# Layer 0 attention: copies between maxima and exponents, routing roots for two batches at once, and every variance root as exp(-0.5 ln v) with a Newton step

## The chip, the cores and the metric

One core of one Trainium2 chip runs the whole program. The metric is the device time of one execution in microseconds (us); lower is better. The unchanged kernel takes 1991.19 us, the median of three runs (1990.56 to 1992.09).

## The reference, cut to what matters

Four layers, each a gated cross attention and then a gated mixture of experts, over 8 batches of 256 tokens with 256 features:

```python
x = x + tanh(g_xattn[n]) * attention_n(layernorm(x), ctx)
x = x + tanh(g_ffn[n])   * experts_n(layernorm(x))
def _layernorm(x, axis=-1, eps=1e-05):
    return (x - m) / jnp.sqrt(v + eps)       # m, v: mean and variance over the features
# layer 0 attention: 16 heads of 16 features, a mask of its own for each batch
scores = jnp.einsum('bhqd,bhkd->bhqk', q / 4, k)
scores = jnp.where(mask[:, None, :, :], -1e30, scores)
out = jnp.einsum('bhqk,bhkd->bhqd', softmax(scores), v)
# experts: the router picks 2 of 8 experts for every token from layernorm(x) @ gate_w.T
```

Every layer norm needs one reciprocal root for each token: of x ahead of each attention and each router, and of the context in layers 1 and 3.

## The kernel before, in words

The layers follow one another, and each half layer is a block of its own in which TensorE (PE), VectorE (DVE), ScalarE (ACT), GpSimd (POOL) and SyncE (SP) each run their own list of instructions, tied by semaphores. The order of work is written out by step. In layer 0 (`packed_attention`) a step is four heads of one batch; four steps make a batch, so 32 steps have scores, and two more finish what is left. Step s = 4b + u does:

- PE: `scores(b, u)` (L2068) into four banks `s_banks`, as soon as `s_free` says that ACT has read the last scores; `weigh` (L2081) the heads of two steps ago; `turn_probs` (L2091), the transposes of the step before, in four turns `pT` 0 to 3; then `turn_back`, the projections of the next batch (`PACKED_STEP`: k at u = 0, x at 1, q at 2, v at 3) and the router's jobs. All these results but the scores go through a ring of four banks `t_ring`, in the order of their numbers: a bank is written again when the result four numbers before has been copied out.
- DVE: `take_max` (L2239) for the four banks, then the copies of turns 2 and 3 (L2246), then v, `move_back` (four instructions for each half of a batch, L2258 to L2265), the mask (L2231), the norms and the router's work.
- ACT: `move_heads` (L2168), `exponent` (L2157, two instructions a bank) for banks 0 and 1, copies of turns 0 and 1 (L2164), `exponent` for banks 2 and 3, which ends with `s_free`; then the copies of the projections, and last `norm.take` or `route.norm.take`.

A root goes through three calls of `Norm`: `ask` on DVE (variance plus eps, L225), `take` on ACT (square root, L232), `scale` on DVE (reciprocal, L238). Ahead of a function that the loaded activation table does not hold, the compiler puts an `ACT_TABLE_LOAD`. It has a record in the trace, under the line of the instruction that it serves. In layer 0 a take ends a step: three times for the x of two batches (`x_stats`, steps 0, 8 and 16), and once for each of the first seven batches for the router (`f_ask`, steps 6, 10, 14 and so on to 30). One more take stands in the opening.

The router's work on DVE (`choose_parts`, a generator with five parts: softmax or sigmoid, first expert, second expert, counts, gates) is done for four batches in steps 23 (three parts) and 24 (the rest), and for two batches in steps 31 and 32. In step 25 ACT scales the rows (L427), and POOL sends them to their slots (L761). `more_turns` names the steps in which ACT takes all four copies.

Layers 1 and 3 (`tiled_attention`) and 2 (`whole_attention`) make takes in the same way, one batch at a time, and each has an extra exponent of one column (`exp_table`) that brings the exponent's table in early. The expert block of layer 0 (`routed_half_layer`) has one take for the last batch, and at its end takes the root of all context variances at once (L3882, L3970).

Of the kernel before, what the change touches and what calls it, by code (L numbers as in the profile page):

```python
# [199 lines left out]

class Norm:

    def __init__(self, nc, ctx, kept, L, twice):
        self.nc, self.kept, self.twice = nc, kept, twice
        self.moments = ctx.enter_context(nc.sbuf_tensor(L + "moments", [P, TILES, 2], F32))
        self.rstd = ctx.enter_context(nc.sbuf_tensor(L + "rstd", [P, TILES], F32))
        self.L = L

    def open(self, tag):

        self.asked = self.kept.semaphore(self.L + tag + "root_asked")
        self.taken = self.kept.semaphore(self.L + tag + "root_taken")
        self.asks, self.takes, self.scales = 0, 0, 0

    def ask(self, step, b0, b1):
# [5 lines left out]
        var, root = self.moments[:, t0:t1, 1], self.rstd[:, t0:t1]  # L221
        if self.twice:
            ins = nc.vector.tensor_scalar(root, var, 1.0 + EPS, EPS * EPS, ALU.mult, ALU.add)
        else:
            ins = nc.vector.tensor_scalar(root, var, EPS, None, ALU.add)  # L225
        ins.then_inc(self.asked, 1)

    def take(self, act, b0, b1):
        root = self.rstd[:, b0 * TB:b1 * TB]
        self.takes += 1  # L230
        act.wait_ge(self.asked, self.takes)
        self.nc.scalar.activation(root, root, ACT.Sqrt).then_inc(self.taken, 1)  # L232

    def scale(self, dve, step, b0, b1):
        root = self.rstd[:, b0 * TB:b1 * TB]
# [32 lines left out]
class Route:  # L268
# [161 lines left out]
    def vector_normed(self, dve, step, b):  # L430
        self.norm.scale(dve, step, b, b + 1)
        if self.cfg.routed and b >= self.cfg.held:
# [396 lines left out]
def tiled_attention(nc, kept, cfg, ctx_in, w, pre, next_weights, head, route, zeroed, shares_out):  # L829
# [131 lines left out]
    with ctx:  # L961
# [23 lines left out]
        exp_table = sb("exp_table", [P, 1])  # L985
# [432 lines left out]
        def _(act):  # L1418
            act.wait_ge(pre.landed, pre.total)
# [70 lines left out]
            nc.scalar.activation(exp_table[:, :], kept.ident[:, 0:1], ACT.Exp)  # L1490
# [295 lines left out]
def packed_attention(nc, kept, cfg, ctx_in, w, pre, next_weights, route, zeroed):  # L1786
# [8 lines left out]
    TURNS = GROUPS  # L1795
    LAG_T, LAG_PV = 1, 2
    RT = 4
    BACK_AT = 1
# [8 lines left out]
    def back_jobs(b, u):  # L1807
        return [("oback", b - 1, t) for t in range(TB)] if u == BACK_AT and 0 <= b - 1 < BATCH else []

    def out_step(e):  # L1810
        return (e + 1) * BLOCKS + BACK_AT

# [2776 lines left out]
```

## Time and profile before

| | |
|---|---|
| Median of three runs | 1991.19 us |
| The profiled execution: its own time | 1999.09 us |
| its span | 1997.4 us |
| granted TensorE clock, mean | 0.941 |
| PE, DVE, ACT busy | 87%, 54%, 39% of the span |

The profiled execution is 7.9 us longer than the median, and its span leaves out 1.7 us of its own time. The layers lie in the span about so: layer 0 attention 0 to 311 us, its experts to 416, layer 1 attention to 682, its experts to 987, layer 2 attention to 1127, its experts to 1460, layer 3 attention to 1884, its experts to the end. In rows of a timeline the first number is the start, the second the time from the start of the first to the end of the last of the merged instructions, and the brackets hold the idle time of that engine just before and what ended it. In rows of busy time by stretch stand the stretch, its length, the busy us of PE, PE's weight loads, DVE, ACT and POOL (each with its count of instructions), the granted clock as a share of 2.4 GHz, the DMA's share and GB/s.

### The profile page before, as it was taken

To read this page: it belongs to the slowest core of one execution; us is meant where nothing else is said; L and a number is where in the kernel's file an instruction comes from. 1 tells how busy PE (TensorE), PEld (TensorE's weight loads), DVE (VectorE), ACT (ScalarE), POOL (GpSimd) and SP (SyncE) were. 2 spreads that over 40 slices of the span, in tenths; PEclk is the share of its full clock that TensorE was granted. 3 is DMA by queue.
4 is the path that set the end of the run, shared out by engine and by line. 5 is a ranking of instruction groups with operands and counts; after the bars stand their busy time and mean duration, and the time that the engine had idled before them with its cause. 6 is when DMAs were issued, how large, how long until landed. Compare 5 with 4: busy or idle time off the path is not lost. (4 is left out here: it accounts for less than half of the span.)

```text
span 1997.4 us, 28170 instructions
## 1 busy us (share of the span) xinstructions
PE 1740.5 (87%) x9431; PEld 1264.5 (63%) x9431; DVE 1070.9 (54%) x3135; ACT 776.4 (39%) x1785; POOL 258.6 (13%) x277
## 2 busy tenths in 40 slices
PE   6888658879989899999848689999979999999796
PEld 4656545656757567888737558888645665656563
DVE  4867655647667462323238554101346767676564
ACT  5777763355555311111125312221124444444321
POOL 2100112031020120000141130000040001010232
PEclk9988878989999899999969789999989999999898
DMA  7644003311111322545334558334222111110452
GB/s 230 218 141 156 32 13 110 88 55 38 33 54 54 116 90 93 178 149 168 119 118 143 188 184 281 128 111 136 99 76 75 41 41 51 30 48 12 130 160 77
DMA packets 170925, 212.91 MB, mean 107 GB/s; under 512 B 17081, under 2 KB 137506, under 8 KB 170658
## 3 DMA queue, kind: packets, MB, share of 16 engines
q1 hardware_dynamic: 159730, 183.57, 28.9%
q0 software_dynamic: 10496, 27.28, 4.3%
q8 instruction: 80, 1.31, 0.3%
q14 instruction: 59, 0.48, 0.1%
q10 hardware_dynamic: 560, 0.27, 0.0%
HBM read 148.95 MB, written 57.92 MB: 104 GB/s over the span
## 5 line engine op out<-in xcount | busy, mean ns | idle before, releaser
L761 POOL DMA_INDIRECT slots_in<-f_xn,f_slot x88 | 85.5, 971 | 501.8 <-DVE f_slot L538 478.0
L3459 PE MATMUL r_bank<-r_w,r_hT 128*128 x624 | 139.3, 379 | 1.0 <-DVE r_hT L3603 1.0
L3459 PEld LDWEIGHTS r_bank<-r_w,r_hT 128*128 128x128 f32 x624 | 118.4, 190 | 22.8 <-issue 7.5
L1321 PEld LDWEIGHTS a_t<-kept_ident,a_probs 128*128 128x128 f32 x768 | 83.9, 143 | 66.0 <-issue 42.5
L2239 DVE CUSTOM_DVE_ANT_0 a_s<-a_s,a_mask_bias 128x256 f32<-128x256 f32 x256 | 99.6, 461 | 44.1 <-PE a_s L2068 37.1
L1471 ACT ACTIVATE a_probs<-a_s,a_negmax 128x512 f32<-128x512 f32 x128 | 86.9, 684 | 92.4 <-DVE a_negmax L1720 92.3
L1305 PE MATMUL a_s<-a_kT,a_qT 64*128 64x256 f32 (+1 forms) x512 | 110.6, 531 | 10.7 <-ACT a_probs L1477 5.1
L3074 PE MATMUL r_bank<-r_xgT,r_firsts 128*128 128x256 f32 x512 | 113.2, 379 | 0.0
L1321 PE MATMUL a_t<-kept_ident,a_probs 128*128 128x128 f32 x768 | 107.3, 283 | 5.4 <-ACT a_probsT L1495 3.4
L1720 DVE TENSOR_REDUCE a_negmax<-a_s 128x1 f32<-128x512 f32 x128 | 82.2, 684 | 51.4 <-PE a_s L1305 48.3
L3544 DVE TENSOR_TENSOR r_y<-r_bank,r_b_row 128x256 f32<-128x256 f32 (+1 forms) x27 | 14.7, 544 | 177.1 <-PE r_bank L3459 176.5
L2157 ACT ACTIVATE a_probs<-a_s,a_negmax 128x256 f32<-128x256 f32 x256 | 102.3, 501 | 7.9 <-DVE a_negmax L2239 7.8
L1338 PE MATMUL a_o_bank<-a_probsT,a_v 128*64 128x256 f32 x768 | 99.8, 396 | 5.8 <-ACT a_o_raw L1524 4.4
L3074 PEld LDWEIGHTS r_bank<-r_xgT,r_firsts 128*128 128x128 f32 x512 | 96.0, 190 | 12.4
L1738 DVE COPY a_probsT<-a_t 128x512 f32<-128x512 f32 x146 | 93.5, 681 | 0.7 <-PE a_t L1321 0.6
L3511 ACT ACTIVATE r_hT<-r_bank,f_b_of 128x256 f32<-128x256 f32 x96 | 45.5, 474 | 116.5 <-PE r_bank L3432 116.5
L1245 PE MATMUL a_s<-a_xT,kept_weights 128*128 128x256 f32 x384 | 87.8, 382 | 0.0
L3432 PE MATMUL r_bank<-r_xgT,r_firsts 128*128 128x256 f32 x384 | 84.9, 379 | 0.0
L782 POOL DMA_INDIRECT g_y_got<-slots_out,kept_y_slot x32 | 30.6, 957 | 411.9 <-POOLq L3290 263.0
L3159 ACT ACTIVATE r_s_silu<-r_bank 128x256 f32<-128x256 f32 x64 | 24.6, 384 | 149.2 <-PE r_bank L3074 149.2
L2091 PE MATMUL a_t<-kept_ident,a_probs 128*128 128x128 f32 x512 | 68.0, 285 | 15.6 <-ACT a_o_raw L2168 13.7
L1245 PEld LDWEIGHTS a_s<-a_xT,kept_weights 128*128 128x128 f32 x384 | 72.3, 193 | 10.6 <-issue 1.3
(427 smaller groups left out, 3548.5 us busy)
## 6 DMA issues: line engine op xcount, KB each, us to landing
r_firsts<-in_f_w SPq DMA_DIRECT2D x27, 1024.0 KB, 5.1
r_firsts<-in_f_w SPq DMA_DIRECT2D x46, 512.0 KB, 4.4
slots_in<-a_zeros SPq DMA_DIRECT2D x8, 2048.0 KB
half_in<-a_zeros SPq DMA_DIRECT2D x8, 1024.0 KB
r_w<-in_f_w SPq DMA_DIRECT2D x8, 1024.0 KB
a_share_of<-shares_out SPq DMA_DIRECT2D x28, 256.0 KB, 3.9
r_xg<-slots_in SPq DMA_DIRECT2D x28, 256.0 KB, 3.5
slots_out<-r_y SPq DMA_DIRECT2D x28, 256.0 KB
```

What stands on the lines that cost most here:

```text
L761: pool.indirect_dma_start(self.slots_in[:, :], bass.IndirectOffsetOnAxis(ap=self.slot[:, c, tile:tile + 1], axis=0), src, None).then_inc(s ...
L1245: last = nc.tensor.matmul(out, weight[:, k, c * P:(c + 1) * P], src[:, k, :], start=(k == 0), stop=(k == DK - 1))
L1305: last = nc.tensor.matmul(out, qT[rows, e % 2, m, c, t * P:(t + 1) * P], kT[rows, e % 2, c, :], start=True, stop=True)
L1321: last = nc.tensor.transpose(bank[:, n * P:(n + 1) * P], src, ident[:, :])
L1338: last = nc.tensor.matmul(o_bank[g * R:(g + 1) * R, 0:SEQ], v[:, e % 2, kt, h, :], probsT[:, half, i, kt, :], start=(kt == 0), stop=(kt == ...
L1471: last = nc.scalar.activation(probs[:, g % PROBS, i, :], bank[:, :], ACT.Exp, bias=negmax[:, g % 4, i, 0:1], accum_out=sum_of(e, h, t_only))
L1738: nc.vector.tensor_copy(turned(e, w_, i), t_bank(n)[:, :].rearrange("p (k n) -> p k n", k=KT)).then_inc(t_free, 1)
L2157: last = nc.scalar.activation(probs[:, u % 2, g, cols], s_banks[g][:, cols], ACT.Exp, bias=negmax[:, u % 2, g, t:t + 1], scale=-1.0)
L2239: last = nc.vector.tensor_tensor_reduce(out=cols, in0=cols, in1=mask_bias[:, e % 2, t, :], scale=-1.0, scalar=3e38, op0=ALU.add, op1=ALU.m ...
L3074: last = nc.tensor.matmul(b_bank(n)[:, i * 2 * P:(i + 1) * 2 * P], firsts[:, j % RW, i, k, m * P:(m + 1) * P], xgT[:, j % 2, k, :], start= ...
L3432: last = nc.tensor.matmul(bank[:, 0:2 * P], slots.firsts[:, j % RW, k, i * P:(i + 1) * P], xgT[:, j % 2, k, :], start=(k == 0), stop=(k == ...
L3459: last = nc.tensor.matmul(d_bank[:, t * D:(t + 1) * D], hT[:, j % 2, m, t * P:(t + 1) * P], slots.second[:, bass.ds(e, 1), m, :], start=(m ...
```

## The change

- `Norm.take` becomes `near_root`: a logarithm, a wait for it, and an exponent with scale -0.5. `Norm.scale` becomes `newton_root`: three DVE instructions instead of one reciprocal. The context's root at the end of layer 0's experts goes the same way.
- `load_exp_table` loads, by name, a table with both logarithm and exponent at the start of ACT's list in layers 1, 2 and 3. The extra exponents of one column go.
- In layer 0 DVE copies turn 0 between maxima 0, 1 and maxima 2, 3, and turn 3 after them; ACT copies turn 1 between its exponents and turn 2 after them.
- In layer 0 the router's take is made for two batches at once, and a take stands in the next step, behind `move_heads` and ahead of the exponents. `choose_parts` is spread over three steps. `turn_back` and `move_back` do one half of a batch in step u = 1 and the other at u = 2. There is one step more.

```diff
+def load_exp_table(nc):
+    nc.scalar.preload_act_table_set("natural_log_exp_and_others")
+def near_root(nc, act, root, var, logs, count):
+    nc.scalar.activation(root, var, ACT.Ln).then_inc(logs, 1)
+    act.wait_ge(logs, count)
+    return nc.scalar.activation(root, root, ACT.Exp, scale=-0.5)
+def newton_root(nc, step, root, var, spare):
+    step(nc.vector.scalar_tensor_tensor(out=spare, in0=root, scalar=-0.5, in1=root, op0=ALU.mult, op1=ALU.mult))
+    step(nc.vector.tensor_tensor(spare, spare, var, ALU.mult))
+    step(nc.vector.scalar_tensor_tensor(out=root, in0=spare, scalar=1.5, in1=root, op0=ALU.add, op1=ALU.mult))
...
-        self.nc.scalar.activation(root, root, ACT.Sqrt).then_inc(self.taken, 1)
+        near_root(self.nc, act, self.rstd[:, tiles], self.var[:, tiles], self.logs, self.takes).then_inc(self.taken, 1)
...
-        step(self.nc.vector.reciprocal(root, root))
+        newton_root(self.nc, step, self.rstd[:, tiles], self.var[:, tiles], self.moments[:, tiles, 1])
...
# tiled_attention, block.scalar (layers 1 and 3); whole_attention (layer 2) has the same ahead of its first move
+            load_exp_table(nc)
             act.wait_ge(pre.landed, pre.total)
-            nc.scalar.activation(exp_table[:, :], kept.ident[:, 0:1], ACT.Exp)
...
# packed_attention (layer 0)
-    BACK_AT = 1
+    BACK = {1: 0, 2: 1}
...
-    for b in range(route.cfg.last):
-        s = out_step(b) + 1
-        extra[s].append(("f_ask", b, 0))
-        extra[s + 1].append(("f_normed", b, 0))
-        extra[s + 2].append(("f_turn", b, 0))
-        extra[s + 3].append(("f_logits", b, 0))
+    SOON = route.choose_groups[-2][0]
+    for b0 in range(0, route.cfg.last, 2):
+        b1 = min(b0 + 2, route.cfg.last)
+        s = out_step(b1 - 1)
+        extra[s].append(("f_ask", b0, b1))
+        extra[s + 1].append(("f_scale", b0, b1))
+        for b in range(b0, b1):
+            extra[s + 1].append(("f_normed", b, 0))
+            extra[s + 2].append(("f_turn", b, 0))
+            extra[s + (3 if b >= SOON else 5 + b - b0)].append(("f_logits", b, 0))
     for k, (b0, b1) in enumerate(route.choose_groups[:-1]):
-        s = out_step(b1 - 1) + 5
+        s = out_step(b1 - 1) + (4 if b1 > SOON else 7)
         extra[s].append(("f_exp", b0, k))
-        extra[s + 1].append(("f_choose", b0, k))
-        extra[s + 2].append(("f_gates", b0, k))
-        extra[s + 3].append(("f_count", b0, k))
+        for n, parts in enumerate((2, 2, 1)):
+            extra[s + 1 + n].append(("f_choose", k, parts))
+        extra[s + 4].append(("f_count", b0, k))
...
-            nc.scalar.activation(exp_table[:, :], kept.ident[:, 0:1], ACT.Exp)
             for s in range(STEPS):
...
                 if block_of(s, LAG_PV):
                     move_heads(*block_of(s, LAG_PV))
+                for kind, e, n in extra[s - 1]:
+                    if kind == "x_stats":
+                        norm.take(act, e, e + 2)
+                    elif kind == "f_ask":
+                        route.norm.take(act, e, n)
...
# DVE in layer 0
                 if b < BATCH:
-                    for g in range(GROUPS):
-                        take_max(b, u, g)
-                if turned:
-                    for i in range(ACT_TURNS[turned], TURNS):
+                    take_max(b, u, 0)
+                    take_max(b, u, 1)
+                if 0 not in by_act:
+                    move_turned(*turned, 0)
+                if b < BATCH:
+                    take_max(b, u, 2)
+                    take_max(b, u, 3)
+                for i in range(1, TURNS):
+                    if i not in by_act:
                         move_turned(*turned, i)
...
# end of layer 0's experts
-            nc.scalar.activation(kept.ctx_rstd[:, :], kept.ctx_rstd[:, :], ACT.Sqrt).then_inc(c_taken, 1)
+            near_root(nc, act, kept.ctx_rstd[:, :], c_var[:, :], c_logs, 1).then_inc(c_taken, 1)
...
-            nc.vector.reciprocal(kept.ctx_rstd[:, :], kept.ctx_rstd[:, :])
+            newton_root(nc, step, kept.ctx_rstd[:, :], c_var[:, :], c_spare[:, :])
```

`packed_attention` has no call of `load_exp_table`, nor has any expert block.

## Rows read from the trace of the kernel before

**Rows 1.** Busy time by stage: layer 0's steps, layers 1, 2 and 3 attention.
```profile
24.00:262.00 238.00, 181.01 (x1569) 132.46 (x1567) 163.73 (x666) 172.72 (x396) 26.98 (x30) 0.89 0.44 142
...
417.00:700.00 283.00, 258.30 (x1455) 182.69 (x1454) 183.89 (x484) 147.18 (x418) 49.34 (x52) 0.95 0.20 58
...
985.00:1127.00 142.00, 96.92 (x459) 80.08 (x459) 79.44 (x287) 56.54 (x122) 46.05 (x48) 0.83 0.39 121
...
1460.00:1830.00 370.00, 346.92 (x1841) 219.21 (x1840) 247.96 (x534) 164.15 (x379) 39.28 (x41) 0.98 0.16 45
```

**Rows 2.** Timeline of PE, a plain step of layer 0 (scores to scores).
```profile
48.98 1.15 PE L2068 MATMUL a_s<-a_kT,a_qT 32*128 32x256 f32 x16
50.05 1.07 PE L2081 MATMUL a_t<-a_probsT,a_v 128*32 128x256 f32 x16
51.05 1.97 PE L2091 MATMUL a_t<-kept_ident,a_probs 128*128 128x128 f32 x16
53.66 1.97 PE L2037 MATMUL a_t<-a_c_turned,kept_weights 128*128 128x256 f32 x8 [0.64 <-ACT a_probsT L2164]
55.55 1.15 PE L2068 MATMUL a_s<-a_kT,a_qT 32*128 32x256 f32 x16
```

**Rows 3.** Timeline of ACT, the same step.
```profile
51.46 1.58 ACT L2157 ACTIVATE a_probs<-a_s,a_negmax 128x256 f32<-128x256 f32 x4
52.90 1.10 ACT L2164 COPY a_probsT<-a_t 128x512 f32<-128x512 f32 x2
53.84 1.63 ACT L2157 ACTIVATE a_probs<-a_s,a_negmax 128x256 f32<-128x256 f32 x4
```

**Rows 4.** Timeline of DVE, the same step: fourth and last of eight maxima, copies.
```profile
51.22 0.47 DVE L2239 CUSTOM_DVE_ANT_0 a_s<-a_s,a_mask_bias 128x256 f32<-128x256 f32 x1
...
53.13 1.28 DVE L2246 COPY a_probsT<-a_t 128x512 f32<-128x512 f32 x2
```

**Rows 5.** Timeline of ACT, a step of layer 0 with a take.
```profile
138.11 1.28 ACT L232 ACT_TABLE_LOAD   x1
139.41 0.20 ACT L232 ACTIVATE f_rstd<-f_rstd 128x2 f32<-128x2 f32 x1
...
139.89 1.28 ACT L2157 ACT_TABLE_LOAD   x1
```

**Rows 6.** Busy time from scores to scores, steps 7, 23, 24 and 27.
```profile
69.47:78.76 9.29, 6.23 (x58) 4.33 (x57) 4.31 (x18) 8.97 (x18) 0.00 (x0) 1.00 0.61 177
...
204.26:215.19 10.93, 7.71 (x57) 5.38 (x57) 3.17 (x16) 10.09 (x21) 0.00 (x0) 0.84 0.00 1
215.19:228.55 13.36, 8.58 (x62) 6.29 (x61) 11.61 (x54) 6.12 (x15) 0.00 (x0) 0.74 0.01 1
249.20:269.89 20.69, 8.43 (x57) 5.72 (x56) 4.88 (x18) 9.09 (x18) 8.40 (x9) 0.67 0.10 32
```

**Rows 7.** DVE groups with shapes apart, 24 to 262 us: busy us, mean ns.
```profile
L2263 DVE SCALAR_TENSOR_TENSOR kept_x<-a_o,kept_tanh_g,kept_x 128x256 f32<-128x256 f32 x12 | 6.0, 498 | 0.4
...
L2258 DVE RECIPROCAL a_rsums<-a_t 128x16 f32<-128x16 f32 x12 | 3.1, 256 | 4.0 <-PE a_t L2099 3.8
```

**Rows 8.** Timeline of DVE: two small dependent instructions of a choice, in order.
```profile
218.30 0.22 DVE L490 TENSOR_TENSOR f_cand<-f_sel,f_top 128x64 f32<-128x64 f32 x1
218.56 0.22 DVE L491 SCALAR_TENSOR_TENSOR f_cand<-f_cand,kept_counting 128x64 f32<-128x64 f32 x1
```

**Rows 9.** Timeline of DVE and PE at the end of layer 0's experts.
```profile
414.70 0.25 DVE L3970 RECIPROCAL kept_ctx_rstd<-kept_ctx_rstd 128x16 f32<-128x16 f32 x1 [5.00 <-ACT kept_ctx_rstd L3882]
...
416.38 1.12 PE L1239 MATMUL a_s<-kept_ident,kept_weights 128*128 128x128 f32 x4 [3.86 <-DVE kept_weights L1550]
```

**Rows 10.** Timeline of PE, layer 1 attention: idle time after a take.
```profile
443.14 1.69 PE L1305 MATMUL a_s<-a_kT,a_qT 64*128 64x256 f32 x8 [2.05 <-ACT a_probs L1477]
...
496.01 1.13 PE L1305 MATMUL a_s<-a_kT,a_qT 64*128 64x256 f32 x8 [0.84 <-issue]
```

**Rows 11.** Timeline of PE, layer 2 attention.
```profile
1088.62 1.07 PE L2495 MATMUL a_s<-kept_ident,a_xn 128*128 128x128 f32 x4 [2.26 <-DVE a_xn L241]
```

More of the change, by code:

```diff
@@ L1807, in back_jobs @@
     def back_jobs(b, u):
-        return [("oback", b - 1, t) for t in range(TB)] if u == BACK_AT and 0 <= b - 1 < BATCH else []
+        return [("oback", b - 1, BACK[u])] if u in BACK and 0 <= b - 1 < BATCH else []
     def out_step(e):
-        return (e + 1) * BLOCKS + BACK_AT
+        return (e + 1) * BLOCKS + max(BACK)
     extra = defaultdict(list)
@@ L1851, in packed_attention @@
         if turned:
-            ACT_TURNS[turned] = 4 if s in more_turns else 2
+            ACT_TURNS[turned] = (0, 1, 2, 3) if s in more_turns else (1, 2)
             for i in range(TURNS):
@@ L2167, in move_heads @@
                 bank = full(act, t_at["o", e, u])
-                nc.scalar.copy(o_raw[:, u, :], bank[:, 0:SEQ]).then_inc(t_moved, 1)
+                nc.scalar.copy(o_raw[:, (e * BLOCKS + u) % OUTS, :], bank[:, 0:SEQ]).then_inc(t_moved, 1)
             move("k", 0)
@@ L2182, in _ @@
                     exponent(b, u, 1)
-                if turned:
-                    move_turned(*turned, 0)
-                    move_turned(*turned, 1)
+                for i in by_act:
+                    if i < 2:
+                        move_turned(*turned, i)
                 if b < BATCH:
@@ L2188, in _ @@
                     exponent(b, u, 3)
-                if turned:
-                    for i in range(2, ACT_TURNS[turned]):
+                for i in by_act:
+                    if i >= 2:
                         move_turned(*turned, i)
@@ L2257, in move_back @@
                 heads = full(dve, n)[:, :].rearrange("p (h r) -> p h r", h=H)
-                step(nc.vector.reciprocal(rsums[:, t, :], heads[:, :, DV]))
+                step(nc.vector.reciprocal(rsums[:, :], heads[:, :, DV]))
                 nc.vector.tensor_tensor(o[:, :].rearrange("p (h d) -> p h d", h=H), heads[:, :, 0:DV],
-                                        rsums[:, t, :].unsqueeze(2).to_broadcast([P, H, DV]), ALU.mult).then_inc(t_free, 1)
+                                        rsums[:, :].unsqueeze(2).to_broadcast([P, H, DV]), ALU.mult).then_inc(t_free, 1)
                 taken(dve, n)
@@ L2270, in route_job @@
                 if kind == "f_ask":
-                    route.norm.ask(step, e, e + 1)
+                    route.norm.ask(step, e, k)
+                elif kind == "f_scale":
+                    route.norm.scale(dve, step, e, k)
                 elif kind == "f_normed":
-                    route.vector_normed(dve, step, e)
+                    route.vector_xn(dve, e)
                 elif kind == "f_logits":
@@ L2279, in route_job @@
                 elif kind == "f_choose":
-                    if k == 0:
-                        dve.wait_ge(route.consts_in, 16 * len(route.consts))
-                        dve.wait_ge(kept.tables_in, 64)
-                    choices[k] = route.choose_parts(dve, step, k)
-                    for _ in range(3):
-                        next(choices[k])
-                elif kind == "f_gates":
-                    for _ in choices[k]:
-                        pass
+                    if e not in choices:
+                        if e == 0:
+                            dve.wait_ge(route.consts_in, 16 * len(route.consts))
+                            dve.wait_ge(kept.tables_in, 64)
+                        choices[e] = route.choose_parts(dve, step, e)
+                    for _ in range(k):
+                        next(choices[e], None)
                 elif kind == "f_count":
@@ L2307, in _ @@
                 turned = block_of(s, LAG_T)
+                by_act = ACT_TURNS[turned] if turned else range(TURNS)
                 if b < BATCH:
-                    for g in range(GROUPS):
-                        take_max(b, u, g)
-                if turned:
-                    for i in range(ACT_TURNS[turned], TURNS):
+                    take_max(b, u, 0)
[7 more added lines that the diff above has]
+                    if i not in by_act:
                         move_turned(*turned, i)
@@ L2662, in _ @@
                     route.norm.take(act, s - 1, s)
-                if s < BATCH - 1:
-                    nc.scalar.activation(exp_table[:, :], kept.ident[:, 0:1], ACT.Exp)
         @block.vector
```

40 lines of the change are left out of this document (20 added, 20 removed).

## The prediction

> **What bounds the kernel now.** I read the busy time by stage first. In layer 0's steps PE works 181 of 238 us, in layer 1 258 of 283, in layer 2 97 of 142; in layer 3 it is nearly full, 347 of 370 [rows 1]. So a shorter ACT or DVE can pay in layer 0, a little in layers 1 and 2, and hardly in layer 3. These PE sums include time at the lower clock (0.89 granted in layer 0), so an idle PE costs twice: the wait itself, and slower matmuls behind it.
>
> The timelines of one plain step of layer 0 show the loop. Scores start at 48.98, weigh ends near 51.1, and the next scores start at 55.55: 6.57 us a step [rows 2]. ACT, after its copy of the heads, does four exponents from 51.46, two copies from 52.90 and four exponents from 53.84 to 55.47, without a gap; that end is what lets the next scores go [rows 3]. PE also waits 0.64 us for ACT's copy of turn 0 before its projection, which ends at about the same time [rows 2]. DVE ends its eight maxima at about 53.2 and its two copies at 54.4, earlier than ACT needs [rows 4]. So a plain step is ACT's chain: 2.2 us of PE (scores, weigh) and 4.3 us of ACT.
>
> A step with a take has more on that chain: a load of 1.28, a root of 0.20, and after the copy of the heads another load of 1.28 [rows 5]. ACT has no free time around them, so the take costs 1.28 + 0.20 + 1.28 = 2.8 us. From scores to scores, steps 7 and 23 take 9.29 and 10.93 us for 6.57, and step 15 is like step 23 (10.8); in these two the clock is 0.84 instead of 1.00, so the work behind the idle time runs slower [rows 6].
>
> **The change, part by part.** All of the sum is in us, against the profiled execution.
>
> *Takes in layer 0.* The router's seven takes become four; the three for x stay. Ten stalls become seven. I take the three that go to be worth what steps 7, 15 and 23 cost over a plain one: 2.7 + 4.3 + 4.4 = 11.4 less [rows 2, 6]. Of the seven that stay, each now has logarithm and exponent together. No row shows a logarithm. The bounds for its table: it shares one with the exponent and nothing is loaded (0), or it has a table of its own and the exponent must load again (2 x 1.28) [rows 5]. The change names the joint table in layers 1 to 3 and nowhere in layer 0, and in the trace each load stands ahead of the one instruction that wants it, first for the root, then for the exponent; a logarithm that finds the exponent's table loaded is nearest to that root. I take the upper end: 1.28 + 0.20 + 1.28 + 0.20 + about 0.25 for the wait between the two = 3.2, for 2.8 now. Seven times 0.4 is 3 more.
>
> The Trainium skill (ScalarE: Activation LUTs, section Table sets: the hidden batching unit) says that a logarithm and an exponent need one load, as one table has both; by that these takes would cost one load at most, and none once that table is in. It is the first rival below. The same page (What ACT_TABLE_LOAD costs) gives 1283 ns for a load and about 1380 ns of drain with it; the trace agrees with the load and shows no drain, since the root's start, 139.41, is 0.02 us after the load's end [rows 5]. With the drain each take here would cost twice as much; the sum goes by the rows.
>
> *Order of copies in layer 0.* ACT's chain loses one copy of the two: from 52.90 to 53.84 two copies took 0.94, so 0.47 less. DVE takes turn 0 in between. Its fourth maximum ends at 51.69, and PE has turned turn 0, a quarter of the 1.97, at about 51.6, so it waits for next to nothing; the copy adds 0.64, the last maximum ends at 53.9, and ACT can end its exponents at 55.0 instead of 55.47 [rows 2, 3, 4]. ACT's copy of turn 2 falls behind the exponents, where ACT has 2.2 us until the next weigh. PE's own work in a step is 1.07 + 1.00 + 1.87 + 1.97 = 5.9, so the step can go to 6.1 and PE is close behind. Where the cover is gone is DVE: it now has about 1.6 us free in a step (from 54.6 until the next maxima near 56.2), and `move_back` with its four instructions of 0.26 to 0.50 for one half, 1.6 in all [rows 7], the norms and the mask must go in there. Splitting `move_back` over two steps helps just that. At a low clock PE turns later, DVE waits for turn 0, and the gain is lost. Bounds: nothing, and 0.47 + 0.3 in each of 31 steps (24). I take 24 plain steps at 0.42: 10 less.
>
> *Choices spread.* Step 24 takes 13.36, 6.8 over a plain one, of which DVE is busy 11.6 [rows 6]: three parts of the choice stand ahead of the maxima. Two, two and one part in three steps are some ten, fifteen and five instructions, each dependent one at most 0.26 from the next, so about 2.7, 3.3 and 1 us [rows 8], and part of it lies under a take's stall in step 27. Bounds: nothing, and the 6.8. I take 3 less. Scaling and scatter of these rows go from step 25 to 29. There is a stall beside them, step 27 with 20.69 [rows 6], in which POOL issues its scatters and all engines stand; I let it move along unchanged.
>
> *Opening and tail of layer 0.* The first take gets a load (1.28), an exponent with its wait (0.45), and `newton_root` two instructions more at the spacing of small ones (2 x 0.26 = 0.5) [rows 5, 8]: 2.2; I take 2 more, as x, its turn, q and the first scores hang on it. The added step holds half of a `move_back`: 1 more.
>
> *End of layer 0's experts.* DVE waits 5.0 us for the root, and the next layer's PE 3.9 us for what follows [rows 9]. The load and the root grow by the same 1.28 + 0.45, the newton step by 0.5: 2 more, all exposed. The named load that opens layer 1 lies under the wait for the first turned context. The take for the last batch in this block costs as many loads as root and router's exponent now.
>
> *Layer 1.* Without loads a take costs 0.45 instead of 2.8. PE waits 2.05 behind the first and 0.84 behind each of six others (one of six shown) [rows 10], and about 0.4 behind the exponent of one column: 2.05 + 6 x 0.8 + 0.4 = 7 less. Two newton steps a batch are 0.9 us of DVE, hidden, with DVE at 184 of 283 [rows 1].
>
> *Layer 2.* Loads lie in ACT's free time; DVE gets 0.9 us a batch more and is waited for in two steps (2.26 in one) [rows 11]. I take 1.5 more; bounds 3 less (the root comes 1.3 sooner in some) and 7 more (eight batches at 0.9).
>
> *Layer 3.* PE is full [rows 1]. Only the opening has the load exposed: 1 less.
>
> Sum: -11.4 + 3 - 10 - 3 + 2 + 1 + 2 - 7 + 1.5 - 1 = -22.9. The profiled execution would go from 1999.1 to about 1976; the median from 1991.2 to 1968.
>
> **The rivals.**
>
> *Layer 0 loads no table.* The logarithm gets the table that also has the exponent. Then the seven takes cost 0.65 instead of 3.2, which is 18 less, some 6 less for the clock (steps 15 and 23 lose 1.6 each to it), and the opening and the end of the experts 1.3 less each: -27 more, 1941 us. For it: the change names such a table elsewhere. Against it: it has to be named in three layers. The Trainium skill (ScalarE activation tables: per-element evaluation and per-set limits, section Table sets in the compiler and the runtime) says that the back end picks the table for the longest run, which would be this one; no row shows how it was picked.
>
> *DVE becomes the bound in layer 0: slower.* If turn 0 is not ready when DVE comes to it, or DVE's extra work outruns its 1.6 us, the maxima of banks 2 and 3 come late by the copy (0.64) and more. The place is L2239's second half; the point is a DVE that ends its extra work later than 1.6 us after its last copy in most steps. At 31 x 0.64 = 20 more instead of 10 less, the sum is +7: 1998. For it: DVE works 164 of 238 us already, in waits for single small instructions. Against it: two of the three kinds of extra work fall in steps with a take, where DVE has 3 us of room.
>
> *Hardly anything gained: the stalls grow with PE's clock.* Takes now stand behind the heads' copy, so PE runs out of work in one long piece. If each of the seven costs 1.6 more and the order gives 3 only, the sum is -5: 1986.
>
> **How the numbers follow.** My case: 0.65. No loads: 0.13. DVE bound: 0.08. Hardly any: 0.14. The forecast is that of the first, 1968, whose own range by the bounds is 1953 to 1980. The range goes up to 1986 for the last rival, and down to 1941 for the first. A measurement of this kernel can tell about 0.2% (4 us) from no change; faster by more than that has 0.65 + 0.13 and half and more of the last: 0.86; within 0.2%: 0.06; slower: 0.08.
>
> **What would show it.** Table loads under L232's successor: two for each of eight takes in layer 0, none in the attentions of layers 1 to 3 but the three named. Plain steps of 6.1 us. Seven steps of 9 to 10.5. In layer 1 no idle PE behind takes. First idle time behind the experts of layer 0 near 6 instead of 3.9. Wrong would make it: a single table in layer 0, DVE's maxima waiting on L2246, or the stall beside the scatters (some 9 us here) growing, going, or falling in the tail where nothing covers it.

## The result, and the profile after

The changed kernel takes 1981.26 us, the median of five runs (1978.12 to 1984.15), where the kernel before took 1991.19: ratio 0.9957, 95% interval 0.9936 to 0.9977. The medians are 9.9 us apart; by the ratio it is 0.43% of 1991.19, 8.6 us, for a forecast of 22.9. The sign and the range held; the size was a good third of the forecast. The profiled pair shows 1997.4 and 1982.0 us of span, 15.4 less, because the profiled execution of before was 7.9 above its median and that of the changed kernel 2.5 above its own.

The busy time by stage, for layer 0's steps and the attentions of layers 1, 2 and 3, in the columns of [rows 1]:

```profile
27.00:259.00 232.00, 194.51 (x1774) 144.29 (x1773) 186.90 (x750) 184.12 (x440) 16.27 (x20) 0.91 0.45 142
405.00:684.00 279.00, 256.08 (x1456) 180.88 (x1455) 188.80 (x516) 126.71 (x415) 49.33 (x52) 0.96 0.20 58
969.00:1112.00 143.00, 92.99 (x459) 76.79 (x459) 82.65 (x313) 39.10 (x113) 46.11 (x48) 0.85 0.38 120
1443.00:1813.00 370.00, 343.80 (x1824) 217.08 (x1826) 251.66 (x559) 142.25 (x373) 38.84 (x40) 0.98 0.16 44
```

Layer 0's stretch of scores now ends at 258.6 instead of 290.8. In layers 1 to 3 ACT is busy 17 to 22 us less in each, since the loads are gone, and DVE 3 to 5 us more; the stretches are hardly shorter. Read against [rows 1], ACT's gain there bought almost nothing.

A plain step went as forecast. The timeline of PE, with the step that answers to [rows 2], and ACT's and DVE's of the same step:

```profile
53.90 1.15 PE L2095 MATMUL a_s<-a_kT,a_qT 32*128 32x256 f32 x16 [0.38 <-ACT a_probs L2184]
...
59.96 1.15 PE L2095 MATMUL a_s<-a_kT,a_qT 32*128 32x256 f32 x16 [0.29 <-ACT a_probs L2184]
```
```profile
56.39 1.57 ACT L2184 ACTIVATE a_probs<-a_s,a_negmax 128x256 f32<-128x256 f32 x4
57.82 0.61 ACT L2191 COPY a_probsT<-a_t 128x512 f32<-128x512 f32 x1
58.29 1.62 ACT L2184 ACTIVATE a_probs<-a_s,a_negmax 128x256 f32<-128x256 f32 x4
```
```profile
56.67 0.69 DVE L2274 COPY a_probsT<-a_t 128x512 f32<-128x512 f32 x1
```

From scores to scores it is 6.06 us for 6.57. ACT has one copy between its exponents, and DVE takes turn 0 at 56.67, where the last of the four maxima ends. PE waits 0.29 us only.

A step with a take, ACT's timeline, for [rows 5]:

```profile
87.41 1.28 ACT L208 ACT_TABLE_LOAD   x1
88.70 0.21 ACT L208 ACTIVATE a_rstd<-a_var 128x4 f32<-128x4 f32 x1
88.93 1.28 ACT L210 ACT_TABLE_LOAD   x1
90.22 0.20 ACT L210 ACTIVATE a_rstd<-a_rstd 128x4 f32<-128x4 f32 x1
```

Two loads, one for the logarithm and one for the exponent: 2.9 us from 87.41 to 90.33, where the exponents begin. There are ten pairs in the whole kernel, in all takes of layer 0 and its experts; the loads of the whole kernel fall from 91 to 33. The Trainium skill (ScalarE: Activation LUTs, section Table sets: the hidden batching unit) says that a logarithm and an exponent need one load; here each take had two, until the joint table was named in this block too (one_table, below). Four of the seven steps with a take, 9, 11, 17 and 19, take 9.1 to 9.2 us; step 1 takes 7.2, step 27 9.7, and step 31 lies in the tail. The step behind a take is long too. These are steps 9 and 10, before and after:

```profile
85.78:96.03 10.25, 7.79 (x70) 6.62 (x69) 8.54 (x34) 8.62 (x18) 3.40 (x4) 0.83 0.90 289
96.03:102.68 6.65, 5.93 (x57) 4.30 (x56) 5.87 (x25) 4.37 (x11) 0.00 (x0) 1.00 1.09 384
```
```profile
84.81:93.89 9.08, 5.29 (x57) 3.71 (x57) 8.80 (x35) 7.97 (x18) 2.73 (x4) 0.96 0.84 264
93.89:102.89 9.00, 9.00 (x61) 6.44 (x61) 6.15 (x24) 5.42 (x13) 0.48 (x1) 0.66 1.09 386
```

Before, the low clock (0.83) fell into the step of the take, and the next ran at 1.00. Now PE is busy for the whole of step 10, at 0.66.

The end of layer 0, first ACT's timeline, then PE's:

```profile
258.79 0.36 ACT L437 ACTIVATE f_score<-f_score 128x32 f32<-128x32 f32 x1
274.95 0.37 ACT L2195 COPY a_o_raw<-a_t 128x256 f32<-128x256 f32 x1 [15.80 <-remote]
```
```profile
275.38 1.12 PE L2118 MATMUL a_t<-kept_ident,a_probs 128*128 128x128 f32 x4 [12.84 <-ACT a_o_raw L2195]
283.47 1.94 PE L2108 MATMUL a_t<-a_probsT,a_v 128*32 128x256 f32 x16 [6.97 <-ACT a_probsT L2191]
...
299.86 2.90 PE L3772 MATMUL r_bank<-f_xT,r_sw 128*128 128x512 f32 x3 [6.96 <-PEq L1896]
```

ACT, PE and DVE come to stand one after another, for 15.8, 12.8 and 12.4 us. ACT is the first to go on, 2.5 us after the end of the last of POOL's 16 scatters (start 271.46, 0.96 long); PE waits for ACT's copy of the heads, and DVE for ACT's root. `remote` means that no instruction of this core ended ACT's wait. Before, this stall stood in step 27 [rows 6]; now it stands in the tail.

The difference of the spans, stage by stage, from the first scores and the first matmul of each block. The last two columns are pairs from the experiments below: the same two kernels on another chip, and both with pauses in POOL's trains on a chip where no engine stands beside them.

| us, after less before | forecast | first pair | before_again, after_again | before_paused, after_paused |
|---|---|---|---|---|
| up to the first scores | +2 | +5.2 | +4.1 | +4.5 |
| first scores to those of step 31 | -21.4 | -37.4 | -42.7 | -29.8 |
| from there to layer 0's experts | +1 | +18.6 | +18.7 | +2.7 |
| layer 0's experts | +2 | +1.7 | +3.0 | +1.0 |
| layer 1 attention | -7 | -4.0 | +0.3 | 0.0 |
| layer 1 experts | 0 | 0.0 | -2.2 | +1.7 |
| layer 2 attention | +1.5 | +1.3 | +2.1 | -0.5 |
| layer 2 experts, layer 3 attention | -1 | -0.7 | +9.2 | +3.5 |
| layer 3 experts | 0 | 0.0 | +0.3 | +1.2 |
| sum | -22.9 | -15.4 | -7.3 | -15.7 |

### The profile page after: what moved, and what is told of

It reads as the page before. It is cut to its first block and busy times, and to the rows that moved or that the text cites. A ratio compares the mean times of both kernels' runs of the same rounds, so it can differ in the third digit from the quotient of the medians.

```text
span 1982.0 us, 28263 instructions
## 1 busy us (share of the span) xinstructions
PE 1728.0 (87%) x9431; PEld 1254.7 (63%) x9431; DVE 1090.1 (55%) x3245; ACT 709.2 (36%) x1771; POOL 258.2 (13%) x277
## 5 line engine op out<-in xcount | busy, mean ns | idle before, releaser
L1344 PEld LDWEIGHTS a_t<-kept_ident,a_probs 128*128 128x128 f32 x768 | 83.6, 142 | 65.3 <-issue 43.7
L3105 PEld LDWEIGHTS r_bank<-r_xgT,r_firsts 128*128 128x128 f32 x512 | 96.0, 190 | 12.4
L2118 PEld LDWEIGHTS a_t<-kept_ident,a_probs 128*128 128x128 f32 x512 | 61.4, 152 | 29.4 <-issue 15.5
L1268 PEld LDWEIGHTS a_s<-a_xT,kept_weights 128*128 128x128 f32 x384 | 72.1, 192 | 10.4 <-issue 1.3
```

Of the source, the lines that this page charges most:

```text
L1268: last = nc.tensor.matmul(out, weight[:, k, c * P:(c + 1) * P], src[:, k, :], start=(k == 0), stop=(k == DK - 1))
L1344: last = nc.tensor.transpose(bank[:, n * P:(n + 1) * P], src, ident[:, :])
L2118: last = nc.tensor.transpose(bank[:, (kt * TB + t) * P:(kt * TB + t + 1) * P], probs[:, u % 2, i, t * SEQ + kt * P:t * SEQ + (kt + 1) * P] ...
L3105: last = nc.tensor.matmul(b_bank(n)[:, i * 2 * P:(i + 1) * 2 * P], firsts[:, j % RW, i, k, m * P:(m + 1) * P], xgT[:, j % 2, k, :], start= ...
```

## The experiments

The kernels ran in batches, each on one chip. What can be compared directly is what ran in one batch, or ratios to the kernel before; differences in us below are of medians. The kernel before took 1910.46 in the first batch, 1999.5 in the second, 1990.87 in the third, 1999.59 in the fourth and 1909.98 in the fifth.

**The two halves apart.** `order_only` is the kernel before with the new `packed_attention`; `roots_only` the changed kernel with the old one:

```diff
 # order_only: Norm, layers 1 to 3 and the experts as before
-def packed_attention(...)   # before
+def packed_attention(...)   # after, takes by Sqrt and reciprocal
 # roots_only: the reverse, in the changed kernel
```

> The kernel before with the changed kernel's layer 0 loop alone (order of copies, halves of the move back, paired takes behind the heads' copy, spread choices); all roots stay square root and reciprocal. By the terms of the prediction: -11.4 - 10 - 3 + 1 = -23 us against the kernel before. By the theory that the stall beside the 16 scatters has moved to the tail and takes back there what the steps gained: about -12. If the steps' gain is worth nothing outside layer 0: 0.

> The changed kernel with layer 0's attention loop as it was before (copies, moves back, router's seven takes and the choice in their old places); all roots stay as logarithm, exponent and a Newton step. By the terms of the prediction: ten takes at +0.4, opening +2, end of the experts +2, layer 1 -7, layer 2 +1.5, layer 3 -1 = +1.5 us against the kernel before. By what the two traces show (first scores 5.2 later, layer 1 only 4 shorter, layer 3 2.4 longer): +6 to +10. If the new roots gained anything by themselves it would be below 0.

order_only: 1883.83, ratio 0.9866 (0.9844 to 0.9888), 26.6 us less. roots_only: 1922.92, ratio 1.0064 (1.0049 to 1.0079), 12.5 us more. The new order alone gives what the forecast had for it (23.4) and a little over; the new roots, for which its terms made +1.5, are a loss of 12.

**The table loads of layer 0.**

```diff
 # packed_attention, @block.scalar
 def _(act):
+    load_exp_table(nc)
     act.wait_ge(pre.landed, pre.total)
```

> The changed kernel with one line more: ACT names the joint table of logarithm and exponent at the start of layer 0's attention too. If the two loads of each take there are what they seem, loads fall from 34 to about 15, the seven steps with a take go from 9.1 to about 6.7 us, the first scores come 1.3 earlier, and the time falls by 7 x 2.4 + 1.3 + 2.6 (take of the last two batches) + 1.3 (context's root) = about 22 us against the changed kernel, 1959. The rival: what the steps gain is swallowed by the stall beside the scatters, which then falls at another place in the tail or grows; then no more than 10 us are gained.

> The joint table named in layer 0 too, now beside the changed kernel itself. Expected against it: 22 to 28 us less (seven takes of the loop at 2.6 to 3.0, opening 5, the last take 2.6, the context's root 1.3), on either kind of chip. If the stall beside the scatters swallows part of it, under 15 where the stall occurs.

> The changed kernel, unchanged, as the common base of this batch. On a chip on which the kernel before takes about 1910 and no engine stands beside GpSimd's trains: 0.9926 (order_only -26.6 and roots_only +12.4 added). On one where it takes about 1995: 0.995 to 0.998, as twice before.

one_table: 1868.89, ratio 0.9782 (0.9769 to 0.9794). one_table_b: 1952.63, ratio 0.9813 (0.9791 to 0.9835); after_b beside it 1980.66, ratio 0.9954 (0.9936 to 0.9972), so the line is worth 28.0 us. In its profile no take has a load, and the loads of the whole kernel fall from 33 to 14. In one_table the first scores start at 20.75 instead of 26.2 in window4 (below) of the same batch. The rival of the prediction had priced this at 27 less than its own case. The total was right, in part by luck: by the profiles of window4 and one_table, layer 0's steps are 18.9 us shorter for its 24, the opening 5.4 for 1.3, and the tail, for which it had nothing, 3.3.

```diff
 # roots_one_table: the same line in roots_only
```

> The changed kernel's roots with the joint table named in every layer, and layer 0's loop as before. Against the kernel before the loads of ten takes go in layer 0. By one_table less order_only's gain: -41.6 + 26.6 = -15 us if the two parts add; if the loads cost more in the old order (a take in the middle of ACT's chain), -20 to -28. If the new roots were a loss by themselves even without loads, above 0.

1980.79, ratio 0.9911 (0.9889 to 0.9934), 18.7 us less than the kernel before: with all loads named, the new roots pay in the old order too. (The expectation's -20 to -28 was a little too much, its -15 too little.)

**The Newton step.**

```diff
 # no_newton: one_table, and in Norm.scale and at the end of the experts
-newton_root(self.nc, step, self.rstd[:, tiles], self.var[:, tiles], self.moments[:, tiles, 1])
 # newton_twice: one_table, and in newton_root
+for _ in range(2):
     step(...)  # the three instructions
```

> The changed kernel with the joint table named in layer 0 too (as in one_table) and without the Newton step: each root is what the exponent gives. Theory A, the three dependent instructions of the Newton step (one reciprocal before) hold up the maxima behind them in layer 3, 0.6 to 0.7 us in one step of each batch, and so layer 3 is 6 to 8 us longer than with square roots: against one_table's ratio 0.9782 this one is 0.4 to 0.7% lower (0.972 to 0.974), and the wait of 0.59 behind the exponents goes. Theory B, layer 3 is longer for the wait between logarithm and exponent on ACT: the ratio stays within 0.1% of one_table's.

> one_table with the Newton step done twice at each of the 58 roots: three more small dependent instructions of DVE each, some 0.2 us apart. Theory A, that these instructions lie on the path that sets the end in layers 1, 2 and 3 as the runs without the step suggest (layer 3 9 to 12 us shorter there, layer 1 6 to 8, layer 2 5): each layer gets about as much longer again, 25 to 35 us against one_table in all. Theory B, that what the runs without the step gained is something else (a wait for the logarithm's semaphore, the order of waits): under 10.

In no_newton each root is what logarithm and exponent give, so it leaves out a part of the arithmetic. no_newton: 1948.14, ratio 0.9751 (0.9731 to 0.977). newton_twice: 1987.19, ratio 0.9983 (0.9971 to 0.9994), 34.6 us more than one_table_b in its batch, and 27.4 by the spans of the two profiles. The price of three such instructions at 58 roots depends on how it is taken. Added, it is 34.6. Taken away, it is less: 0.9751 stands against 0.9782 in one_table (6 us) and 0.9813 in one_table_b (12 us), both in other batches, and no_newton is 45.9 under after_again in its own batch, of which the table's 28.0 leave 18. The 0.972 to 0.974 that was expected wasn't reached. By the profiles the extra step made layer 1's attention 6.0 us longer, layer 2's 8.4, layer 2's experts with layer 3's attention 11.5; no_newton, on another chip, has 6.0, 5.8 and 5.4 less there than one_table_b. These are the two kernels' rows from layer 2's experts to the end of layer 3's attention (first newton_twice, then one_table_b):

```profile
1111.80:1871.20 759.40, 697.84 (x3468) 491.89 (x3469) 397.90 (x1021) 231.60 (x558) 71.36 (x74) 0.97 0.31 98
```
```profile
1095.50:1843.40 747.90, 695.05 (x3467) 490.41 (x3468) 391.34 (x970) 231.49 (x558) 71.60 (x74) 0.97 0.31 100
```

DVE has 51 instructions and 6.6 us more, and PE, doing the same work, arrives 11.5 us later; ACT's work is unchanged. So what newton_twice adds is not the logarithm's wait. The place can be seen in layer 3 on the first batch's chip. DVE's timeline of one step in order_only, then in roots_only:

```profile
1546.56 0.69 DVE L1631 COPY a_v<-a_t 128x512 f32<-128x512 f32 x1 [2.25 <-PE a_o_bank L1341]
1547.17 0.15 DVE L238 RECIPROCAL a_rstd<-a_rstd 128x2 f32<-128x2 f32 x1
1547.36 0.74 DVE L241 TENSOR_SCALAR a_xn<-kept_x,a_moments,a_rstd 128x256 f32<-128x256 f32 x2
1548.01 0.16 DVE L238 RECIPROCAL f_rstd<-f_rstd 128x2 f32<-128x2 f32 x1
1548.21 0.74 DVE L241 TENSOR_SCALAR f_xn<-kept_x,f_moments,f_rstd 128x256 f32<-128x256 f32 x2
1548.86 1.28 DVE L1723 TENSOR_REDUCE a_negmax<-a_s 128x1 f32<-128x512 f32 x2
```
```profile
1588.49 0.69 DVE L1651 COPY a_v<-a_t 128x512 f32<-128x512 f32 x1 [2.25 <-PE a_o_bank L1361]
1589.10 0.15 DVE L215 SCALAR_TENSOR_TENSOR a_moments<-a_rstd 128x2 f32<-128x2 f32 x1
1589.29 0.16 DVE L216 TENSOR_TENSOR a_moments<-a_moments,a_var 128x2 f32<-128x2 f32 x1
1589.48 0.16 DVE L217 SCALAR_TENSOR_TENSOR a_rstd<-a_moments,a_rstd 128x2 f32<-128x2 f32 x1
1589.68 0.74 DVE L262 TENSOR_SCALAR a_xn<-kept_x,a_moments,a_rstd 128x256 f32<-128x256 f32 x2
...
1591.57 1.28 DVE L1743 TENSOR_REDUCE a_negmax<-a_s 128x1 f32<-128x512 f32 x2
```

Both roots of a batch are scaled in one step, ahead of that step's maxima. From the copy of v to the maxima it was 2.30 us and is 3.08. The exponents wait for the maxima, and PE for them. PE's timeline of roots_only, 2.3 us behind:

```profile
1593.88 1.13 PE L1328 MATMUL a_s<-a_kT,a_qT 64*128 64x512 f32 x4 [0.59 <-ACT a_probs L1495]
```

The scores that answer to it in order_only (1551.17) start with no wait. It is 0.78 us on DVE, and 0.78 from one start of PE's scores to the next, of which 0.59 shows as a wait. Five of layer 3's eight batches have this wait of 0.59 in roots_only, window4 and one_table; in order_only and no_newton none has it, and in newton_twice it is 1.18 in four, with 4.25 from the copy to the maxima.

**The stall beside the scatters.** The page of the second batch showed it again, and the first batch's did not:

> The kernel before, unchanged, profiled on the chip of the runs beside it. In an earlier batch the kernel before took 1910 us where it took 1991 in the first result, and its variants there had none of the long idle times beside the scatters and gathers. If that is a matter of the chip, this profile has idle times of PE of over 6 us beside GpSimd's 16 scatters in layer 0 and 32 gathers in layer 2 only when its time is near 1990; near 1910 it has none.

> The changed kernel, unchanged, beside the kernel before. From order_only (-26.6) and roots_only (+12.4), if the two parts add, -14 us, ratio 0.9926. If the share that the stall beside the scatters takes is what made the first result small, then on a chip without it the gain is that of order_only less the roots, over 10 us; if the stall plays no part, -8.5 as in the first result.

before_again, one execution: 2001.57. Its PE stands 8.10 us beside the scatters of layer 0 and 17.80 beside the 32 gathers of layer 2. after_again: 1993.99, ratio 0.9973 (0.9953 to 0.9992), with 7.1 and 19.1. In the profiles of the first batch, window4 with its pauses apart, PE has no such idle time behind a train: step 27 takes 10.98 in roots_only, 20.69 in [rows 6]. It goes with the chip. That answers what before_again asked; after_again, 5.5 less than the kernel before, stays under both the 14 and the 8.5 of its expectation.

```diff
 # pool_scatter, for the first group of layer 0
+if k == 0 and self.relu2 and sent and sent % 4 == 0:   # sent: scatters issued so far
+    pool.wait_ge(self.scattered[0], 16 * sent)
+sent += 1
 pool.indirect_dma_start(self.slots_in ...)
```

> The changed kernel, where GpSimd waits after every fourth of the 16 scatters of the first four batches until they have landed. Theory A, the engines stand because scatters are queued faster than they drain: the 12.8 us in which PE stands in the tail shrink to 4 or less, the train gets up to 8 longer, and the time falls by 5 to 9 us. Theory B, the stall comes from something else in the tail (the take, a semaphore, the low clock) : the same 12 to 13 us stay and the time is within 3 us.

> The changed kernel with a wait of GpSimd after every fourth of the first 16 scatters until they have landed, now beside the changed kernel. On a chip where no engine stands beside the scatters: the same time, within 2 us. On one where they do, theory A (scatters are queued faster than they drain): PE's 7 to 13 us before its transposes in the tail shrink below 4 and the time falls by 4 to 9; theory B (the train's length alone, or each scatter as such): PE stands as long or longer, and the time is the same or up to 6 longer.

window4, on the chip without the stall: 1899.69, ratio 0.9936 (0.9922 to 0.995), and there was no changed kernel beside it. window4_b, on one with it: 1971.89, ratio 0.9901 (0.9882 to 0.992), 8.8 us less than after_b. Its POOL timeline, and PE's behind the train:

```profile
255.21 0.95 POOL L789 DMA_INDIRECT half_in<-f_xs,f_slot  x1 [0.30 <-issue]
258.20 0.96 POOL L789 DMA_INDIRECT half_in<-f_xs,f_slot  x1 [2.04 <-DMA half_in<-f_xs,f_slot]
```
```profile
262.12 0.66 PE L2122 MATMUL a_t<-kept_ident,a_probs 128*128 128x128 f32 x4 [0.98 <-ACT a_o_raw L2199]
270.20 1.93 PE L2112 MATMUL a_t<-a_probsT,a_v 128*32 128x256 f32 x16 [7.43 <-ACT a_probsT L2195]
```

Three pauses of 2.04 us in the train, and PE's wait of 11.64 in after_b is 0.98. The 7.43 stays (6.96 in after_b): that is the take with its loads and the heads' exponents, with nothing else left for PE.

**The parts together.** best is no_newton with window4's pauses, so it leaves out the Newton step too; best_all also pauses in all scatter trains and after every fourth gather ahead of the attentions of layers 2 and 3:

```diff
 # pool_gather
+if e > 0:
+    pool.wait_ge(self.gathered[(e - 1) % self.ring], 16 * 2 * TB * ((e - 1) // self.ring + 1))
```

> The changed kernel, unchanged, as the base of this batch. On a chip where no engine stands beside GpSimd's trains (kernel before near 1910): 0.9926, from order_only and roots_only there. On the other kind (kernel before near 1995): 0.995 to 0.998, as three times before.

> The changed kernel with three edits: the joint table named in layer 0, no Newton step, and a wait for the landing after every fourth of the first 16 scatters. If the parts add (28 for the loads, 20 to 25 for the Newton step, 9 for the pauses where engines stand beside the scatters): 55 to 62 less than the changed kernel on a chip with the stall, ratio to the kernel before 0.966 to 0.970; without the stall 48 to 53 less. If they overlap (the step and the loads hide behind one another): under 45.

> As best, with pauses in every scatter train and after every fourth gather of the trains ahead of the attentions of layers 2 and 3 too. Theory A, one cause: on a chip with the stall, PE's idle time of 17 to 23 us in layer 2's attention and the 5 to 8 us at the start of layer 3's go below a third, and the time falls by another 20 to 30 us. Theory B, those waits are for the gathered rows themselves: they stay or grow by the pauses, and the time rises by up to 10. On a chip without the stall: the same or up to 5 more, for the pauses.

after_c: 1990.33, ratio 0.9956 (0.9937 to 0.9974). best: 1932.9, ratio 0.9653 (0.9625 to 0.9681), 57.4 us under it, where 55 to 62 was expected if the parts add: they do, within the spread of the Newton step's price. best_all: 1895.17, ratio 0.9472 (0.9444 to 0.9499), another 37.7. PE's idle time in layer 2's attention, after_c's timeline:

```profile
1017.22 3.78 PE L2558 MATMUL a_t<-kept_weights,a_cT 128*128 128x256 f32 x8 [18.01 <-ACT a_cT L2647]
```

In best_all the longest wait of PE in that attention is 2.7 us, although the pauses make the train longer, and the attention is 26.6 us shorter than in best. It was not the gathered rows that the engines waited for. In the tail of layer 0 best_all loses 6.7 us: there the experts wait for the paused last train.

> The kernel before with a pause of GpSimd after every fourth scatter and every fourth gather ahead of the attentions. Theory A (trains longer than some ten indirect transfers make the engines stand): on a chip with the stall 35 to 45 us less than the kernel before, ratio 0.978 to 0.983, and no idle time of PE over 6 us behind a train; on a chip without it 0 to 5 more. Theory B (only the changed kernel's order makes the pauses pay): within 10.

> The same pauses in the changed kernel. If the stall, moved into layer 0's tail where nothing covers it, is what made the change's gain small, this one is 14 to 20 us faster than before_paused. If the gain is small for the Newton step and the loads alone, the difference between the two stays that of the kernels without pauses, 8 to 10 us.

> best_all without the pauses in layer 0's last scatter train (there the experts' start waits for the train: PE's idle time ahead of them was 13.7 us for 7.0) and with pauses in the 24 gathers of the last layer. Expected 5 us from the first edit; from the second 5 less if PE stands beside those gathers (idle times of 4 to 8 us there), or up to 5 more if the end waits for the last gather. Ratio 0.942 to 0.945 if both gain, 0.947 if they cancel.

This batch fell on a chip without the stall. before_paused: 1927.45, ratio 1.0095 (1.0075 to 1.0115); after_paused: 1915.7, ratio 1.004 (1.0024 to 1.0056). The pauses cost the kernel before 17.5 us there, not 0 to 5. PE's idle time ahead of layer 0's experts, 4.16 in the first profile of before, is 12.75, behind the last scatter train; that is half of the 17.5, and the rest was not traced. after_paused is 11.7 under before_paused, between the 8 to 10 and the 14 to 20 that its expectation set apart. best_mixed: 1869.14, ratio 0.9798 (0.9779 to 0.9817). Without pauses in the last train its tail of layer 0 takes 24.0 us, where after_paused's takes 34.0. Its last block, from the first matmul of layer 3's experts, takes 105.3 us (1759.4 to 1864.7) where after_paused's takes 94.1, so pauses in the last 24 gathers lose here. Whether they gain on a chip with the stall wasn't tried.

## Why the prediction was right or wrong

**The step that failed** is "Two newton steps a batch are 0.9 us of DVE, hidden", and with it the 1 less of layer 3 ("PE is full"). The 0.9 was about right, and the overlap was wrong: in layer 3 the two roots of a batch cost 0.78 us more, and it is not hidden. The averages of [rows 1] (DVE 184 of 283) were read as room. But the instructions stand ahead of maxima that the exponents and then PE wait for, in one step of a batch, and there no room is. It holds even with PE at 347 of 370: a full PE has no cover behind it, so what delays it is added.

What the new roots did can be read in one batch, on a chip without the stall. window4 and order_only have the same loop in layer 0, and differ in the roots and in the pauses of one train. By stage, in us:

| window4 less order_only | forecast | measured |
|---|---|---|
| opening | +2 | +4.8 |
| layer 0's steps | +3 | +1.8 |
| from step 31 to layer 0's experts | 0 | 0.0 |
| layer 0's experts | +2 | +1.9 |
| layer 1 attention | -7 | -2.2 |
| layer 1 experts | 0 | +1.3 |
| layer 2 attention | +1.5 | +1.9 |
| layer 2 experts, layer 3 attention | -1 | +8.0 |
| layer 3 experts | 0 | -1.5 |
| sum | +0.5 | +15.9 |

Layer 3 misses by 9.0, layer 1 by 4.8, the opening by 2.8. Of layer 3's attention (7.8), five batches at 0.78 are 3.9, and its first 90 us give another 2.3; those and the remaining 1.6 were not taken apart.

How much of it is the Newton step is known roughly. There are 58 of them, each two instructions longer than a reciprocal. Two thirds of the prices above are 23 us by newton_twice's median, 18 by its profile, and 4 to 12 by taking the step away; the forecast held 0.5 in the opening, 0.5 behind the experts and 1.5 in layer 2. The higher price comes from a second step on top of the first, and need not hold for the first.

**Layer 1's loads** were sized about right, and the Newton step ate much of the gain: without it (no_newton) layer 1's attention is 257.7 us where before_again has 265.8, 8.0 less for a forecast of 7. The changed kernel, four times profiled, has 260.1 to 266.0, so a single pair shows this stage to some 3 us only.

**Layer 0's steps**: right, and better than said. Plain steps 6.06 (6.1 forecast). A take that stays costs 3.0 over a plain step in its own step (9.1 less 6.1), where before it cost 3.7 to 4.4 there, but the low clock has moved into the step behind. Steps 9 to 12 and 17 to 20, four takes with the steps behind them, take 71.3 for 71.9, though eight plain steps are 4.1 shorter: 3.4 more for the four, 2.0 in the paused pair and 0.4 in the other, so 0.1 to 0.9 a take for the 0.4 of the forecast. The three takes that went (steps 7, 15 and 23) are 11.9 shorter, 10.4 without the plain gain, for 11.4. Step 24 takes 6.5, where 13.36 were [rows 6], but part of that comes back in steps 28 to 30 (10.8, 8.8 and 8.9): the six steps 24 to 26 and 28 to 30 are 6.8 shorter, 3.8 without the plain gain, for 3. Without the stall the stretch is 29.8 shorter for 21.4.

**Two loads a take**: right. The take costs 2.9 for 3.2. Of the seven steps of 9 to 10.5, five came.

**Opening**: +5.2 for +2. The root is 3.0 us (14.59 to 17.60) as priced, but PE waits behind it 3.11 for 1.25, and the q projection that follows takes 3.78 us for 1.99, at a granted clock of 0.50 for 1.00; the first context also came 1.1 us later. one_table takes back more than its 2.6 us of loads there, 5.4.

**The stall "moved along unchanged"**: wrong in its place, and smaller in its effect than it looks. The prediction named this itself as a sign of being wrong, "falling in the tail where nothing covers it". Step 27 was 9.7 longer for it (20.69, and 10.98 in roots_only on a chip without it), and the tail is now 14.0 longer (41.3 from step 31 to the experts, and 27.3 in window4 and order_only on that chip). So it took about 4.3 us of the gain. The pair with pauses, which has no stall, is 11.7 us apart by medians, where the plain pairs are 9.9, 5.5, 10.2 and 9.3. The changed kernel itself wasn't timed on a chip without the stall; window4, the nearest to it, is 10.8 less than the kernel before there. So most of the 13 us that are missing would be missing without the stall too.

**Tail**: besides the stall, 27.3 for 22.7: the last take with two loads, and one step more. Forecast +1.

**Rivals.** No loads in layer 0 did not happen, and its total was priced right (27, measured 28.0). DVE as the bound of layer 0 did not happen: with 187 of 232 us it still ends its maxima in time for ACT, whose exponents follow one another without a wait in the step shown above. It did happen elsewhere, in a smaller way, where the forecast had no rival for it. The clock rival's time (1986) is near what came, but for the most part not by its mechanism. A take's stall does put the next step at a low clock (0.66 in step 10), but over both steps it costs 0.1 to 0.9 more and not 1.6; the order gave all of its gain; and the mean clock is 0.941 before and 0.942 after.

The two halves measured apart sum to 14.2 less on a chip without the stall (26.63 less 12.46). How much of the distance from there to the 5.5 to 10.2 of the pairs with the stall is the stall, and how much the spread of a few us between pairs, isn't settled.

## What to carry to other kernels

Price a small instruction by what waits behind it in its own step, not by the engine's busy share over the stage: 0.78 us on a DVE busy for 68% of layer 3 was added in full in five batches of eight. Read the step behind a stall too, for the clock. Name the activation table in every block that mixes logarithm and exponent; one line was worth 28 us here. Where GpSimd issues 16 or more indirect transfers in a row, compare with a version that waits for them four at a time, and do so on more than one chip.

## What the runs showed of the hardware

- Beside a train of 16 or more indirect transfers without a pause (1.27 us apart), the other engines come to stand, one after another, 7 to 14 us after its start in the changed kernel (252.27; ACT's last work before the stall ends at 259.15, PE's at 262.54, DVE's at 265.95). The first of them goes on 2.5 us after the end of its last transfer (272.42 and 274.95; before, 260.03 and 262.65). The first result and three of the five batches show it (kernel before 1991 to 2000), two batches don't (1910): 80 to 90 us between chips for the same program, of which the pauses gave back 46.5. With a wait for landing after every fourth transfer it goes, and with it 8.8 us in layer 0 (window4_b) and another 37.7 in best_all; on a chip without it such waits cost the kernel before 17.5. What is short on those chips (instructions, descriptors or something else) was not found.
- The logarithm and the exponent after it each loaded a table, 1283 ns, at all ten takes of layer 0 and its experts, until the joint one was named at the start of layer 0's list; then neither did (one_table_b: 14 loads for 33).
- A stall of PE is paid twice: in step 10 of the changed kernel, behind a take, PE was busy for all of 9.00 us at a granted clock of 0.66, where the same step before took 6.65 at 1.00.
